# Scores of the tile two ahead moved in front of the attention of the next tile, on every engine

## The reference

```python
def _L0_xattn_ref(x, context, Wq, Wk, Wv, Wo, bo):
    ...
    scores = jnp.einsum('bhid,bhjd->bhij', q, k) * scale
    attn = jax.nn.softmax(scores, axis=-1)
    out = jnp.einsum('bhij,bhjd->bhid', attn, v)
    out = out.transpose(0, 2, 1, 3).reshape(B, Sq, h * d)
    return out @ Wo + bo

def _L0_ffn_ref(x, w_gate, w_up, w_down):
    ...
    g = bitlinear(x, w_gate)
    u = bitlinear(x, w_up)
    h = jnp.square(jax.nn.relu(g)) * u
    return bitlinear(h, w_down)
x = x + jnp.tanh(g_xattn[0]) * _L0_xattn_ref(_layernorm(x, axis=-1), ctx_768, L0_xattn_Wq, L0_xattn_Wk, L0_xattn_Wv, L0_xattn_Wo, L0_xattn_bo)
x = x + jnp.tanh(g_ffn[0]) * _L0_ffn_ref(_layernorm(x, axis=-1), L0_ffn_w_gate, L0_ffn_w_up, L0_ffn_w_down)
```

## Time and profile before

| | us |
|---|---|
| median of three runs | 1289.37 (1286.5 to 1291.16) |
| the profiled execution | 1290.45 |
| its span on the core | 1288.6 |
| TensorE matmuls busy | 1215.6 (94% of the span) |
| VectorE busy | 1061.0 (82%) |
| ScalarE busy | 688.9 (53%) |
| GpSimd busy | 306.4 (24%) |

### The profile page before, as it was taken

The page is one execution under the profiler, slowest core; times in us unless marked ns, Lnnn a source line. Parts: engine busy times, 40 slices in busy tenths (PEclk is TensorE's granted clock), DMA queues, the critical chain, the costliest instruction groups (busy, mean ns, idle before and its releaser), DMA issues.

```text
span 1288.6 us, 18673 instructions
## 1 busy us (share of the span) xinstructions
PE 1215.6 (94%) x6040; PEld 785.5 (61%) x6136; DVE 1061.0 (82%) x2142; ACT 688.9 (53%) x782; POOL 306.4 (24%) x278
## 2 busy tenths in 40 slices
PE   7766999999999999999999999999999999999995
PEld 5544566666665666666665666666665666666652
DVE  4966888888889888888888888888889888888873
ACT  3753545555456455565456545555456455565453
POOL 1024122222233222222233222222233222212210
PEclk9887999999999999999999999999999999999998
DMA  9740434322332344322332344322332333322422
GB/s 390 271 143 21 134 84 91 86 70 77 81 86 61 77 116 141 86 65 76 87 85 65 74 124 133 85 68 79 81 85 59 79 90 88 85 67 73 82 58 57
DMA packets 205178, 124.48 MB, mean 97 GB/s; under 512 B 173931, under 2 KB 173931, under 8 KB 202594
## 3 DMA queue, kind: packets, MB, share of 16 engines
q1 hardware_dynamic: 204573, 120.00, 34.3%
q10 hardware_dynamic: 580, 4.20, 1.1%
HBM read 57.86 MB, written 24.35 MB: 64 GB/s over the span
## 4 chain that ended last, share of the span: by engine, by line
PE 81%; DVE 5%; issue 3%; ACT 2%; POOL 1%; DMA 0%; DVEq 0%; ACTq 0%; POOLq 0%; SPq 0%
PE gu_ps L1028 31%; PE o_ps L1013 17%; PE s_ps L56 15%; PE y_ps L1041 15%; PE s_ps L1001 3%; DVE half_max L1112 1%; POOL v_sb L853 1%; ACT v_sb L900 1%; DVE staged L1107 1%; ACT staged L922 0%; POOL probs L863 0%; ACT x_marked L952 0%; DVE stats L1137 0%; DVE x L1135 0%; DVE x_max L1147 0%
## 5 line engine op out<-in xcount | busy, mean ns | idle before, releaser
L1028 PE MATMUL gu_ps<-w_gate,xq_t 128*128 128x512 bf16 x990 | 238.1, 383 | 7.4 <-DVE staged L1107 4.9
L1041 PE MATMUL y_ps<-w_down,hq_t 128*128 128x512 bf16 x1023 | 234.1, 382 | 6.0 <-DMA hq_t<-staged 5.7
L1028 PE MATMUL gu_ps<-w_up,xq_t 128*128 128x512 bf16 x963 | 233.9, 379 | 3.2
L1013 PE MATMUL o_ps<-v_sb,pt_high 128*128 128x512 f32 (+1 forms) x640 | 215.8, 419 | 13.2 <-DVE pt_low L1097 7.8
L952 ACT ACTIVATE x_marked<-centred,x_scale 128x512 f32<-128x512 f32 x64 | 46.2, 722 | 292.5 <-DVE x_scale L1154 292.5
L1107 DVE TENSOR_TENSOR staged<-staged,gu_ps 128x1024 f32<-128x1024 f32 x128 | 155.5, 1215 | 56.6 <-ACT staged L922 56.6
L858 POOL TENSOR_TENSOR rstd<-var_eps,neg_half 128x1 f32<-128x1 f32 x128 | 99.8, 780 | 416.4 <-DVE var_eps L1074 285.2
L56 PE MATMUL s_ps<-a_sb,xf_high 128*128 128x308 f32 x1024 | 187.1, 305 | 0.0
L1041 PEld LDWEIGHTS y_ps<-w_down,hq_t 128*128 128x128 bf16 x1024 | 100.8, 98 | 129.0 <-issue 10.1
L1028 PEld LDWEIGHTS gu_ps<-w_up,xq_t 128*128 128x128 bf16 x1024 | 100.4, 98 | 121.5 <-issue 1.3
L56 PEld LDWEIGHTS s_ps<-a_sb,xf_high 128*128 128x128 f32 x1024 | 159.7, 188 | 5.8 <-issue 0.5
(11 more groups left out here) (106 smaller groups left out, 1440.1 us busy)
## 6 DMA issues: line engine op xcount, KB each, us to landing
xf_sb<-in_x_feat SPq DMA_DIRECT2D x64, 256.0 KB, 2.8
x_sb<-in_x_tok SPq DMA_DIRECT2D x64, 256.0 KB, 2.9
y<-staged SPq DMA_DIRECT2D x64, 256.0 KB, 2.0
staged<-in_wg_t SPq DMA_DIRECT2D x4, 1024.0 KB, 15.2
staged_up<-in_wu_t SPq DMA_DIRECT2D x4, 1024.0 KB, 23.1
staged<-in_wd_t ACTq DMA_DIRECT2D x4, 1024.0 KB, 6.7
a_scr<-a_out SPq DMA_DIRECT2D x12, 308.0 KB, 4.2
a_raw<-a_scr SPq DMA_DIRECT2D x3, 1232.0 KB, 5.4
```

The source lines that it names most:

```text
L1013: last = nc.tensor.matmul(o_ps[:, :], pt[0:rows, P * c:P * (c + 1)], v_sb[0:rows, v, c, :], start=(c == 0 and pt is pt_high and v == 0), s ...
L1028: last = nc.tensor.matmul(gu_ps[:, m, q, :], xq_t[:, s.par(0), c, :], w[:, c, cols], start=(c == 0), stop=(c == DC - 1))
L1041: last = nc.tensor.matmul(y_ps[:, :], hq_t[:, c, :], w_down[:, c, :], start=(c == 0), stop=(c == FC - 1))
```

## The change

Only the order of calls in `step(s)` changes, on four engines; the work, the semaphores and the buffers stay. TensorE calls `make_scores(s, 2)` before `attend(s, 1)`. VectorE does everything for the scores of tile t + 2 before it turns to the attention of tile t + 1. ScalarE calls `exponentials` first and `mark_input` behind `relu_half(s, 1)`. GpSimd calls `normalise` before the second `root`.

```diff
@@ GpSimd, step
+                    if s.has(2):
+                        normalise(s, 2)
                     if s.has(1):
                         root(var2_ready, s, 1, rstd2, var_eps2, rstd2_done)
-                    if s.has(2):
-                        normalise(s, 2)
@@ ScalarE, step
+                    if s.has(2):
+                        exponentials(s, 2)
+                    if s.has(0):
+                        relu_half(s, 1)
                     if s.has(1):
                         mark_input(s, 1)
-                    if s.has(0):
-                        relu_half(s, 1)
-                    if s.has(2):
-                        exponentials(s, 2)
                     if s.has(0):
                         square_half(s, 1)
@@ TensorE, step
                     if s.has(0):
                         gate_up(s, 0)
+                    if s.has(2):
+                        make_scores(s, 2)
                     if s.has(1):
                         attend(s, 1)
-                    if s.has(2):
-                        make_scores(s, 2)
                     if s.has(0):
                         gate_up(s, 1)
@@ VectorE, step
                     if s.has(0):
                         hidden_half(s, 0)
+                    if s.has(2):
+                        top_scores(s, 2)
+                        shift_scores(s, 2)
+                    if s.has(0):
+                        top_half(s, 0)
+                    if s.has(2):
+                        sum_probs(s, 2)
                     if s.has(1):
                         add_attention(s, 1)
                         input_scale(s, 1)
-                    if s.has(2):
-                        top_scores(s, 2)
-                    if s.has(1):
                         unmark_input(s, 1)
-                    if s.has(2):
-                        shift_scores(s, 2)
-                    if s.has(0):
-                        top_half(s, 0)
-                    if s.has(1):
                         hidden_unit_scale(s, 1)
-                    if s.has(2):
-                        sum_probs(s, 2)
                     if s.has(0):
                         hidden_half(s, 1)
                         top_half(s, 1)
```

## The result

| | before | changed |
|---|---|---|
| median, four runs each | 1287.93 us (1286.27 to 1291.16) | 1309.98 us (1300.02 to 1312.27) |
| the profiled execution | 1290.45 | 1311.54 |
| its span | 1288.6 | 1309.7 |

The ratio is 1.0152 [1.0121, 1.0183]: the change makes the kernel 22 us, 1.5%, slower. The forecast was 1317, range 1302 to 1333. One of the four runs of the changed kernel stands 8 us under the other three; I did not find out why.

A forecast was written before the change was run, and what follows sets the result against it. TensorE was taken to bound the kernel before, the chain from scores to turned input the changed one: steady 24.4 + start 3 + turns 0 = 27.4 us on 1290.45, said as 1317 us, 2.1% slower, range 1302 to 1333.

The forecast's parts named there:

- The bound and the slack: Steady step: TensorE never waits in 17.81 us; slack 0.8 before the probabilities' transposes, 3.2 before the turned input.
- The steady sum: Scores' end to next first gate matmul 11.20, step 18.21 against 17.81: 0.40 wait, 61 times, 24.4 us.
- landing to weight load: End of the input's chain: from the landing of the DMA transpose to TensorE, 0.14 us.
- weight load to matmul: Last term of the input's chain, on TensorE: from weight load to first gate matmul, 0.11 us.
- The start: First tiles: first gate matmul at 121.52, the next at 141.56, 2.1 later than before; 3 us taken, up to 3.9.
- The turns: Turns of a batch, six places: scores wait in the attention's place; 0 taken, bounds -5.4 and +4.3 us.
- The hold-ups: VectorE and GpSimd share a port lock; normalising could block `centred` up to 1.22 us a step; nothing taken.
- No steady wait: Rival: hand-over covered, TensorE waits for nothing in the steady run, only the start remains, about 1292; chance 0.10.
- Faster at the turns: Rival: scores ahead of the attention cover the values' conversion, 3 x 1.81 = 5.4 us, giving 1284; chance 0.04.
- The clock: Rival: gaps before each first half bring the clock down, about 1430, or some 1335 at a few places; chance 0.04.
- The second multiplication: Rival: TensorE waits for `gu_ps`, late on VectorE, adding the excess over 0.9 of cover; counted within the forecast's 0.82.
- The Trainium skill's fit of the forecast: Input's DMA transpose: 2.0 us fixed plus bytes, an estimate of 2.3; wait 0.30 a step, result about 1311.

The follow-up runs named there:

- the sum in the gap: Changed kernel with VectorE's sum of the probabilities and reciprocal moved behind the row's scale, while ScalarE rounds, and GpSimd's root before the normalising: 1324.6 us, ratio 1.0279.

## Why the prediction was right, point by point

**The bound and the slack.** TensorE bound the kernel before (0.22 more on it cost 0.22), and the input's chain bounds the changed one (0.6 more on VectorE cost 0.6, 0.22 more on TensorE nothing). This is shown from both sides.

**The steady sum: right in mechanism, the wait twice too large.** Forecast 11.20 from the end of the scores to the gate matmul, 0.40 a step; measured 10.99 and 0.20. The terms 0.04, 0.82, 0.71, 1.13, 0.82, 0.12, 0.19, 0.84, 0.51 and 2.4 came within 0.02 of what was measured. Two did not: landing to weight load 0.06 instead of 0.14, and weight load to matmul 0.01 instead of 0.11. Both had been taken from other places, and one span was counted twice. The 0.14 of the earlier trace rows ends at the matmul, as its heading says: the landing is at 1278.62, the weight load starts at 1278.73 and the matmul at 1278.76. It holds the step from weight load to matmul already, and the sum then added 0.11 for it, from a weight load that waited for nothing, beside matmuls of the block before. Add to scale took 3.33 instead of 3.37. The step that failed is thus "from the landing to TensorE 0.14 ... and from weight load to matmul 0.11", 0.18 of the 0.21; 0.11 of it the double count. A wait that is the small difference of two sums of 18 doubles with it. The term is 10.4 over the 54 ordinary steps, and 0.40 would have made 21.6. The range of 0.25 to 0.55 a step did not reach to 0.20. That the total still lies in its range is in part luck: the steady term was some 12 too high, and the turns, taken at 0, brought 6 back.

**The start.** The first gate matmul comes at 122.15, forecast 121.52; tile 1's at 141.14, forecast 141.56; tile 2's is 3.74 behind that of before, where 3 and one 0.40 make 3.4. The way there was another than the forecast's. Before, the first gate matmul came at 120.83 although the input of tile 0 was on its way from 115.34 on; it stood behind the transposes of the probabilities (119.28 to 120.61). Now it waits for the input. So it moved by 1.32 only and not by the input's 3.43, and 0.35 of this is not the change's, since VectorE came free at 110.88 instead of 110.53. The clock took 1.10 of the first block (4.71 against 3.61), not 1.83, and tile 1 is 1.70 behind, under the forecast's 2.1; then it fell again in tile 1's wait and the step behind took 19.86:

```profile
141.14 5.31 PE gu_ps L1028 x16
```

The fall in the longer wait (3.37) is what the upper bound had. The start itself moves from one execution to the next by more than this: over all kernels here, none of which changes the stage ahead of the tiles, the first gate matmul came between 115.86 and 124.22.

**The turns.** Forecast 0, bounds -5.4 and +4.3; measured 7.3, of which 1.2 is the six steps' 0.20: 6.1, over the upper bound. The step of the prediction that failed here is "ScalarE's second square, and with it each conversion, moves later by up to the rounding's 0.72, while the step is 0.40 longer. I take 0": the key conversion did move 0.73 later into the step (0.57 ahead of the first gate matmul before, 0.16 behind it now), but the step is only 0.20 longer. The waits are longer by 3 x 0.96 + 3 x 0.26 = 3.7, within it. The rest is the clock, which the bound had left out: behind waits at which it fell the blocks lost 1.5, 1.5 before (5.31 and 5.30 against 3.77 at the second turn) and 1.6, 2.7 and 1.5 after (5.19, 6.31, 5.17 against 3.63), 2.7 more. The two together are 6.4 against 6.1 measured.

**The hold-ups.** `centred` was expected to come as the lock opens: it started at 612.37, GpSimd's normalising had ended at 612.05. Nothing taken for it, and nothing lost.

**The rivals.** No steady wait: false, but only 0.20 from true, nearer than its chance of 0.10 allowed for. Faster at the turns: false as it stands, since `y_scale` holds the split of the probabilities, as the forecast said; with that mended it is true of the values and false of the keys. The clock: not in the steady run, where 0.2 never brought it down; true at tile 1 and at the turns. The second multiplication: not in the changed kernel (it ends at 617.16, 0.8 before the transpose lands), but it is what waits next, as moving the sum showed. The Trainium skill's fit of the forecast ("DMA: Bandwidth & Descriptors", section "Anatomy of one DMA — SWDGE (gpsimd) path"), an estimate of 2.3, would have made the wait 0.30, nearer to the measured 0.20; but the transfer took 2.4 here as well, and the excess lay behind it.

**Left open:** why every fourth step is longer with the sum in the gap; why one execution of the changed kernel was 8 us faster; and why the clock fell behind some waits of about 2 us and not behind others.

## What to carry to other kernels

Before moving a block of the bounding engine, add up the slack of every chain that starts and ends at it: an order that shortens one lengthens another, and here the one with 3.2 us of slack was moved back by 3.4. When the forecast is a small difference between two long sums, price the hand-overs from instructions that wait at that very place, and test it cheaply afterwards by adding a known piece of work to each engine in turn. Look for the stretches in which a one-column product takes microseconds: exchanging it for a one-column tensor_scalar, and cutting a long conversion so that its reader can start on a piece, gave here what no reordering did.

## What the runs showed of the hardware

A tensor_tensor on one column, both inputs in SBUF, takes 0.15 alone and up to 4.37 beside a GpSimd tensor_tensor, ending with it; the same product by tensor_scalar takes 0.20 to 0.21 beside the same instruction. I had not expected the hold-up to pass on whole to the next such product (0.93 on `x_top_sq`). A tensor_scalar over 1024 columns, both ends in SBUF, is held as well: 2.03 instead of 0.69 beside the key subtraction. GpSimd's normalising took 1.36 instead of 1.22 in all runs in which it starts beside `xq`, a tensor_scalar over 512 columns (614.06 for 0.43, normalising from 614.20), the last one with no tensor_tensor beside it included; so the 0.14 is not the price of the held products.

In the changed kernel's steady run the matmul whose weight load has waited follows that load by 0.01; before, in a running queue, it followed by 0.11.

The granted clock fell behind waits of TensorE of 3.00 (two of three), 3.37, 2.06 (one of three) and 2.04 (two of three), never behind the 1.8 of the values before, and never behind 0.2. With all but TensorE changed, waits of 3.5 brought it down in about two steps of three (33 of 23.2, 19 of 21.5), so the length of a wait alone does not tell. A fall cost 1.5 to 2.7 us in the block that followed, 1.7 in a block of gate and up (5.31 against 3.63). Where the clock stayed up, a block behind a wait took no longer than in a running queue. The chain has 3.77 against 3.48 for the attention and 3.63 against 3.40 for the scores only because it counts a running block from the end of the one before; from its own first matmul the attention takes 3.84 before, and the scores 3.75 in the changed kernel.
